# Where TensorE turns the probability blocks in the second attention of layer 0

## The reference

```
xn = rmsnorm(x) * gamma1
q, k, v = xn @ q_w + q_b, xn @ k_w + k_b, xn @ v_w + v_b     # 16 heads x 64
q, k = rope(q), rope(k)
scores = einsum('bhqd,bhkd->bhqk', q, k) / sqrt(64), causal
attn = softmax(scores)
ctx = einsum('bhqk,bhkd->bhqd', attn, v)
attn_out = ctx @ o_w + o_b + xn
```

## Time and profile before

| | before |
|---|---|
| median of the runs | 3685.12 us |
| profiled execution | 3683.81 us |
| its span (first to last instruction) | 3682.0 us |
| mean granted TensorE clock, share of 2.4 GHz | 0.809 |
| busy, whole span: PE, PEld, DVE, ACT, POOL | 2640.1, 1652.8, 1882.2, 1329.0, 768.1 us |
| the changed function's matmuls | from 596.0 to about 1448 us of the span |

### The profile page before, as it was taken

The page is one execution under the profiler, slowest core; times in us unless marked ns, Lnnn a source line. Parts: engine busy times, 40 slices in busy tenths (PEclk is TensorE's granted clock), DMA queues, the critical chain, the costliest instruction groups (busy, mean ns, idle before and its releaser), DMA issues. The chain is left out here.

```text
span 3682.0 us, 45740 instructions
## 1 busy us (share of the span) xinstructions
PE 2640.1 (72%) x16185; PEld 1652.8 (45%) x16185; DVE 1882.2 (51%) x3568; ACT 1329.0 (36%) x2779; POOL 768.1 (21%) x960
## 2 busy tenths in 40 slices
PE   2348887999999996259999946597898564112992
PEld 1124443555555553224444434377887333111882
DVE  3358885666666664433333336792222873650333
ACT  2236664565555554223333343310001452210331
POOL 1331111555555552000000000000000221015331
PEclk8669998999999998579999957855776675555996
DMA  2112110000000000200000021334120003012553
GB/s 61 51 58 36 36 36 30 4 4 4 4 4 1 4 1 20 71 28 13 3 15 6 0 72 54 92 118 118 35 51 5 1 1 103 0 41 64 182 181 94
DMA packets 186340, 156.69 MB, mean 43 GB/s; under 512 B 54442, under 2 KB 166813, under 8 KB 185709
## 3 DMA queue, kind: packets, MB, share of 16 engines
q1 hardware_dynamic: 177386, 142.79, 13.6%
q0 software_dynamic: 4544, 9.35, 0.7%
q10 hardware_dynamic: 4224, 2.10, 0.2%
HBM read 112.12 MB, written 47.22 MB: 43 GB/s over the span
## 5 line engine op out<-in xcount | busy, mean ns | idle before, releaser
L1276 DVE TENSOR_TENSOR x_hg<-x_h,x_g_ps 128x512 f32<-128x512 f32 x248 | 170.7, 688 | 329.2 <-PE x_y_ps L1221 296.8
L938 ACT ACTIVATE a_p<-a_s_ps,a_nmax 128x512 f32<-128x512 f32 (+3 forms) x512 | 268.0, 542 | 129.0 <-DVE a_nmax L854 129.0
L1261 ACT ACTIVATE x_h<-x_h_ps,x_w 128x512 f32<-128x512 f32 x256 | 175.8, 687 | 323.6 <-PE x_g_ps L1217 296.2
L854 DVE TENSOR_REDUCE a_nmax<-a_s_ps 128x2 f32<-128x1024 f32 (+3 forms) x256 | 205.2, 822 | 170.1 <-PE a_s_ps L755 166.6
L1213 PE MATMUL x_h_ps<-x_anT,x_w 128*128 128x512 f32 x512 | 263.1, 597 | 25.4 <-DMA x_gT<-gT_d 24.8
L912 POOL TENSOR_SCALAR a_p<-a_p,a_rden 128x512 f32<-128x512 f32 (+3 forms) x512 | 264.0, 536 | 12.5 <-DVE a_rden L861 12.4
L1221 PE MATMUL x_y_ps<-x_hg,x_w 128*128 128x512 f32 x496 | 253.1, 592 | 0.0
L554 DVE TENSOR_REDUCE a_shift<-a_s_ps 128x2 f32<-128x1024 f32 (+3 forms) x256 | 202.2, 820 | 53.9 <-PE a_s_ps L461 51.8
L768 PEld LDWEIGHTS a_pt_ps<-ident,a_p 128*128 128x128 f32 x1280 | 147.0, 141 | 170.6 <-issue 151.1
L768 PE MATMUL a_pt_ps<-ident,a_p 128*128 128x128 f32 x1280 | 174.1, 275 | 59.9 <-ACT a_e L948 59.9
L948 ACT COPY a_e<-a_pt_ps 128x1024 f32<-128x1024 f32 (+3 forms) x256 | 172.6, 709 | 102.6 <-PE a_pt_ps L768 102.6
(11 more groups left out here) (433 smaller groups left out, 5451.2 us busy)
## 6 DMA issues: line engine op xcount, KB each, us to landing
f_w<-in_wgud SPq DMA_DIRECT2D x39, 768.0 KB
l_band<-in_fir_long SPq DMA_DIRECT2D x16, 768.0 KB
parts_d<-p_parts SPq DMA_DIRECT2D x16, 384.0 KB, 2.5
a_qs<-parts_d SPq DMA_DIRECT2D x96, 64.0 KB
a_ks<-parts_d SPq DMA_DIRECT2D x96, 64.0 KB
sorted_d<-in_fill SPq DMA_DIRECT2D x1, 5031.0 KB
f_xr<-sorted_d SPq DMA_DIRECT2D x39, 129.0 KB
x_w<-in_w SPq DMA_DIRECT2D x8, 514.0 KB
```

The costliest lines, as they stand in the source:

```text
L854: last = nc.vector.tensor_reduce(nmax[g % 4][:, 2 * at:2 * at + 2], s_ps[g % 2][:, :, c:c + width(i)], AX.X, ALU.max, negate=True)
L938: last = nc.scalar.activation(p[g % 4][:, h, c:c + width(i)], s_ps[g % 2][:, h, c:c + width(i)], ACT.Exp, bias=nmax[g % 4][:, col], accum_ ...
L1261: nc.scalar.activation(h[q][:, :], h_ps[q][:, :], ACT.Gelu, bias=weights(i * SLOTS + c, slice(2 * P, 2 * P + 1)))\
L1276: nc.vector.tensor_tensor(hg[q][:, :], h[q][:, :], g_ps[q][:, :], ALU.mult).then_inc(hg_ready, 1)
```

## The change

The call of `transposes(g - 1)` moves from the end of TensorE's step to directly behind the scores. Nothing else changes: the same instructions run with the same waits, and the lists of the other engines are the same.

```diff
@@ -810,6 +810,8 @@
                 n, k = g // 3, g % 3
                 if g + 2 < steps:
                     scores(g + 2)
+                if 1 <= g <= steps:
+                    transposes(g - 1)
                 if k == 0:
                     if n + 2 < n_pairs:
                         project(n + 2, 0)
@@ -825,8 +827,6 @@
                         project_v(n + NB)
                     if n >= NPAIR and n % NPAIR == 0:
                         output(n // NPAIR - 1)
-                if 1 <= g <= steps:
-                    transposes(g - 1)
```

## The result

The changed kernel takes 3845.47 us (median of 4 runs, 3842.15 to 3887.87) against 3685.61 us for the kernel before, a ratio of 1.0459 with an interval of 1.0385 to 1.0534. The profiled execution took 3845.2 us; its span is 3843.5 us, 161.5 us more than the 3682.0 of before. The mean granted clock of the whole span is 0.803 (0.809 before).

What follows compares the result with a forecast made beforehand. A loop through TensorE and ScalarE was taken to set the pace (PV to turn C 4.70 us, period 11.95). 3683.8 + 124 (115 + 7 + 2) + 100 for the clock, with 1.3 more, gave 3909 us; range 3800 to 3985.

Steps and rivals of the forecast that it cites:

- loop and clock together: The forecast itself: longer TensorE-ScalarE loop plus falls of the granted clock, 3909 us, own range 3860 to 3985, chance 0.74.
- rival 1: TensorE's loop lengthens as forecast but the granted clock stays up: 3809 us, chance 0.12.
- The loop: PV to turn C stays 4.70 us through ScalarE; P0 and turn B lengthen the rest: 60 x 1.92 = 115 us.
- The neighbours: Other moves beside the loop: turn A and waits on other engines cost nothing, by_token 7 us, last pairs 2 us.
- Turn B's wait for the copy of turn A: TensorE's turn B needs ScalarE's copy; fits by 0.4 us, so no cost, up to 30 us if off.
- by_token: In seven pairs this TensorE work moves from beside ScalarE's chain to behind turn C: 7 us, between 0 and 14.
- The two pairs near the end with P0 and no PV: On TensorE, P0 moves behind the wait there: 2 x 0.96 = 2 us.
- The clock: TensorE's granted clock falls to 0.50 behind turn C's wait, one low stretch a pair: 60 x 1.66 = 100 us.
- rival 2: Exponentials of B wait for maxima and scores, not copy_v; only P0 counts: 3743 us, 3793 with some low stretches; chance 0.06.

Runs made afterwards that it cites:

- e7: Changed kernel with a second copy of the same tile into a spare tile ahead of copy_v on ScalarE: 3946.05 us.
- e8: Kernel before with a second copy of the same tile into a spare tile ahead of copy_v on ScalarE: 3711.0 us against 3687.5 (1.0066).
- e1: Kernel before with only turn B moved directly behind the scores, in front of PV: 3750.22 us against 3686.67 (1.0169).
- e2: Kernel before with only turn C moved directly behind the scores, in front of P0: 3799.12 us against 3686.67 (1.0298).
- e5: Changed kernel with ScalarE's list turned round, copy of the turned block first and exponentials last: 3656.48 us against 3687.54 for the kernel before (0.9902).
- e3: Kernel before with only turn A moved directly behind the scores, in front of values and P1: 3724.56 us against 3686.67 (1.0099).
- e4: Changed kernel with two extra, overwritten matmuls a pair on TensorE inside turn C's wait, in 52 pairs: 3812.27 us.

## Why the prediction was right

The time lay in the stated range of 3800 to 3985 us, 64 us under the forecast. It did not lie in the narrower range that belonged to the forecast of loop and clock together, 3860 to 3985 us: 3845 stands between that and rival 1 (3809), and the stated range held it because it took rival 1 in. The direction, the loop and its period were right; the size of the clock's term was not. By its own steps:

- **The loop.** Turn C cannot start earlier than 4.70 us behind PV: 4.59 was measured. Turn C to PV 9.17 us: 9.19. Period 13.87: 13.78. Idle time 2.8: 2.82. The term of 115 us is 60 x 1.83 = 110 us. e7 and e8 show that copy_v is in the chain, e1 and e2 that turn B and P0 each add their part, and e5 that the chain is ScalarE's order and not the early turns as such.
- **The neighbours.** Turn A moved at no cost in the whole change, but for a reason that I had only half: I wrote that P1 to PV stays 3.21 us because turn B takes the place of turn A, and e3 shows what happens if nothing does. Turn B's wait for the copy of turn A, which I had within 0.4 us, did not come: the copy ended 5.7 us behind the start of scores A and turn B started 6.8 behind it (1029.68, 1035.39, 1036.52), so it had 1.1 us of cover. by_token was put at 7 us and cost 3.5: an output pair and the by_token pair behind it take 35.10 us together instead of 30.94, 0.5 more than twice 1.83, seven times. The two pairs near the end with P0 and no PV were put at 2 us and cost 3.4 (13.44 us each instead of 11.73).
- **The clock: the step that was mis-sized.** The price of a low stretch was about right (1.66 expected; 1.3 to 1.65 measured for 22 of them, 2.8 to 2.9 for the other four), its number was not: one a pair expected, 60, and 26 came. I had taken the number from gaps in other stages, nearly all of which were followed by the lower level, and set the one counter-example aside. In the changed kernel 34 of 60 waits of exactly the same length were not followed by it. The term is 44 us instead of 100, and the granted clock of the steady stretch 0.96, where 0.87 to 0.9 was expected. What decides which waits are followed stays open.
- The sum with the measured terms is 110 + 3.5 + 3.4 + 44 = 161 us; the span grew by 161.5.

Of the rivals, the clock that stays up (3809) is close to e4, which took 3812 with the wait filled; it was a part of the truth. The chain through the maxima of B (rival 2) does not set this kernel's pace: the maxima of B end at 1038.62, 0.37 us before the exponentials start at 1038.99. It does set the pace of e3. Both prices of rival 2 (3743 and 3793) lie below the stated range, which the prediction said left out only part of it. The page of the Trainium skill that I cited ("TensorE: Matmul & The Clock Gate", section "Why this matters for your kernels") warns only of longer gaps, of over some 3 us. The traces disagree, since 27 of 60 waits of 1.94 us (e2) and 26 of 60 of 2.82 us were followed by the lower level.

That the spread of the changed kernel's runs (3842 to 3888) comes from the number of low stretches is likely, since the slowest run has the lowest mean clock, 0.790 against 0.801 to 0.803. There is no trace of that run, so it stays open.

## What to carry to other kernels

When two in-order engines hand work back and forth, find the loop: the step on one engine from which the other's chain starts, and the step that waits for its end. Work between the two is free up to the chain's length, work outside is paid in full; moving an instruction "earlier" can carry it, or its neighbours, out of the free part. An early producer helps only if the consumer's own list takes it up early too, and a new idle time on TensorE can cost more than its length: here a low stretch took another 1.6 us behind a wait of 2.82 us, and 2.7 us behind one of 3.30.

## What the runs showed of the hardware

Of the waits of turn C, 12 of 54 were followed by the lower level at 1.59 us (e1), 27 of 60 at 1.94 (e2), 26 of 60 at 2.82, 46 of 53 at 3.30 (e7), and none of 53 each at 0.9 us (before), 1.07 (e3) and 1.38 (e8). Length is not all: 1.94 and 2.82 us have the same share, and of the seven waits of 2.82 us behind an output 3 were followed in the changed kernel and all 7 in e7. What else decides is not shown. A low stretch cost 1.3 to 1.65 us in 22 pairs of the changed kernel and 2.8 to 2.9 in four, and 2.6 to 2.8 us in 25 pairs of e7. Putting work that nobody needs into the wait made the kernel 33 us faster.
